# A loop over pairs of strips, written out strip by strip, in the sampling stage of a deformable convolution

## The reference

```
fine_cal  = conv1x1(gn(x) * (attn + 1), select_w)
align     = conv1x1(concat[fine_cal, 2 * coarse_up], offset_w)
om        = conv3x3(align, om_w, om_b)              # 216 channels: 8 groups x 9 taps x (dy, dx, mask)
val       = for each pixel, group and tap: bilinear sample of coarse_up at (y+ky+dy, x+kx+dx), times sigmoid(mask)
aligned   = einsum(val (9 taps x 256 channels), dcn_w) + dcn_b
out       = x + relu(aligned) + fine_cal
```

## Time and profile before

| | |
|---|---|
| median of 3 runs | 3370.52 us (3359.72 to 3374.48) |
| the profiled execution, its own time | 3370.08 us |
| its span in the trace | 3368.4 us |
| TensorE busy, weight loads busy | 3117.9 us (93%), 2697.5 us (80%) |
| VectorE, ScalarE, GpSimd busy | 2515.5 us (75%), 1517.4 us (45%), 335.5 us (10%) |
| mean granted TensorE clock | 0.967 |
| the sampling stage | from about 1205 us to the end |

### The profile page before, as it was taken

How to read it: one execution, slowest core, us unless ns; L and a number is a source line. 1 busy time by engine, 2 the same in 40 slices (tenths; PEclk the granted TensorE clock), 3 DMA queues, 4 the chain that set the end, 5 groups by cost and what they waited for, 6 DMA issues and landing times.

```text
span 3368.4 us, 91473 instructions
## 1 busy us (share of the span) xinstructions
PE 3117.9 (93%) x34242; PEld 2697.5 (80%) x34242; DVE 2515.5 (75%) x4215; ACT 1517.4 (45%) x2787; POOL 335.5 (10%) x445
## 2 busy tenths in 40 slices
PE   8969999999999938999998999998999998999999
PEld 7859999989999827878776777777777786877788
DVE  3427888888888859878776877887787786878782
ACT  0012222222222116656655565665666565656663
POOL 2000000000000001111111111111111111111111
PEclk9979999999999969999999999999999999999999
DMA  5322344333333232322223222223222233322222
GB/s 165 100 88 73 58 69 71 60 47 52 61 58 55 30 60 43 62 58 61 55 62 58 60 54 64 63 53 68 53 60 54 61 65 55 64 55 61 54 62 57
DMA packets 452882, 211.30 MB, mean 63 GB/s; under 512 B 230821, under 2 KB 447541, under 8 KB 452277
## 3 DMA queue, kind: packets, MB, share of 16 engines
q1 hardware_dynamic: 426112, 161.74, 26.6%
q10 hardware_dynamic: 21724, 26.37, 2.4%
q0 software_dynamic: 4608, 16.78, 1.3%
HBM read 104.86 MB, written 55.23 MB: 48 GB/s over the span
## 4 chain that ended last, share of the span: by engine, by line
PE 48%; ACT 7%; issue 6%; DVE 2%; ACTq 1%; SPq 1%; DMA 0%; POOL 0%; DVEq 0%; POOLq 0%
PE eb L1555 26%; PE tb L1113 14%; PE vb L1135 6%; ACT taps_all L1084 2%; ACT res L1142 1%; ACT wtT L1118 1%; ACT om L1040 1%; PE eb L1148 1%; PE tb L1035 1%; ACTq L1006 1%; DVE wt L1107 1%; ACT mask L1049 1%; ACT ot L1153 0%; SPq L1030 0%; ACTq L1435 0%
## 5 line engine op out<-in xcount | busy, mean ns | idle before, releaser
L1555 PE MATMUL eb<-val,wd 128*128 128x256 f32 (+1 forms) x4680 | 1225.7, 385 | 0.0
L1118 ACT COPY wtT<-tb 128x512 f32<-128x512 f32 x1152 | 662.7, 587 | 682.2 <-PE tb L1113 680.8
L1555 PEld LDWEIGHTS eb<-val,wd 128*128 128x128 f32 x4680 | 798.4, 191 | 120.8 <-issue 57.4
L1113 PE MATMUL tb<-ident,wt 128*128 128x128 f32 x4608 | 710.2, 278 | 85.7 <-issue 37.0
L1113 PEld LDWEIGHTS tb<-ident,wt 128*128 128x128 f32 x4608 | 564.7, 143 | 239.6 <-issue 77.1
L1107 DVE TENSOR_TENSOR wt<-taps_all 128x768 f32<-128x768 f32 x768 | 731.4, 994 | 10.4 <-PE tb L1113 2.1
L547 PE MATMUL conv<-fine,wf 128*108 128x256 f32 x4608 | 593.5, 290 | 13.1 <-DVE omT L878 13.1
L547 PEld LDWEIGHTS conv<-fine,wf 128*108 128x108 f32 x4608 | 572.8, 174 | 28.7 <-issue 28.7
L1488 DVE COPY val<-vb 128x432 f32<-128x432 f32 (+1 forms) x384 | 212.7, 554 | 240.4 <-PE vb L1135 240.1
L1135 PE MATMUL vb<-wtT,win 64*32 64x144 f32 x16384 | 323.3, 292 | 60.7 <-issue 56.4
L1135 PEld LDWEIGHTS vb<-wtT,win 64*32 64x32 f32 x16384 | 245.6, 108 | 108.5 <-issue 108.0
(11 more groups left out here) (142 smaller groups left out, 2499.8 us busy)
## 6 DMA issues: line engine op xcount, KB each, us to landing
val<-val SPq DMA_DIRECT2D x128, 396.0 KB, 3.8
win<-cpad SPq DMA_DIRECT2D x304, 64.0 KB
om_s<-om_d SPq DMA_DIRECT2D x1152, 12.0 KB
chunk<-in_x SPq DMA_DIRECT2D x32, 512.0 KB, 5.0
xchunk<-in_x SPq DMA_DIRECT2D x32, 512.0 KB, 4.1
r_d<-r POOLq DMA_DIRECT2D x32, 512.0 KB, 3.2
rt<-r_d SPq DMA_DIRECT2D x63, 256.0 KB, 4.9
out<-ot ACTq DMA_DIRECT2D x63, 256.0 KB, 2.9
```

The lines of the kernel that those rows point to most:

```text
L1113: last = nc.tensor.transpose(tb[b][:, 128 * j:128 * j + 128], wt[half][:, 4 * i + j, :], ident[:])
L1118: return nc.scalar.copy(dst, src) if e == "act" else nc.vector.tensor_copy(dst, src)
L1555: done = nc.tensor.matmul(eb[q][:, 256 * fo:256 * fo + rows], wd[:, half, k, 128 * fo:128 * fo + 128], val[:, half, k, at:at + rows // W, ...
```

## The change

The loop of `loop` goes: all 34 values of `it` are written out, for TensorE, VectorE and ScalarE. Each `strips(it)` issues the same work in the same order as before.

```
             def loop(e, strips):
 
-                strips(0)
-                strips(1)
-                with e.Fori(2, ST // 2 - 1) as it:
-                    strips(it)
-                for it in range(ST // 2 - 1, ST // 2 + 2):
+                for it in range(ST // 2 + 2):
                     strips(it)
```

## The result

The changed kernel takes 3281.79 us (median of 4 runs, 3280.20 to 3283.52) against 3369.99 us before (4 runs, 3359.72 to 3374.48): ratio 0.9743, 95% interval [0.9720, 0.9765], 88 us less. Forecast were 3277 us and a range of 3258 to 3305.

What follows compares the result with a forecast made beforehand. TensorE, busy 3117.9 of 3368.4 us, was taken to set the end. From 3370.1 us, 97.4 for jumps was subtracted and 4 for stops in written-out code added: 3276.7, so 3277 us, range 3258 to 3305.

Steps and rivals of the forecast that it cites:

- steps 1 and 3: TensorE's 28 loop jumps in the sampling stage: 136.4 us excess, of which 97.4 us goes, 3.48 us a jump.
- step 4: Bursts in written-out code on TensorE: 7 or 8 short stops of 0.57 us in 56 strips, adding about 4 us.
- step 2: First strips of images 1 to 3: TensorE's waits for window loads remain, so 39.0 us of the excess stays.
- pairs take over 61.5 us without an image's first strip: Sign in the sampling stage that the prediction is wrong; two strips were expected to take 60.8 us throughout.
- step 5: VectorE and ScalarE lose jumps and register instructions: nothing gained, since TensorE has the work; VectorE's smallest cover is 0.83 us.
- step 3: Sampling stage: 97.4 us goes, covering both gaps, the slow clock behind them and few jumps with another engine late.
- step 6: SyncE and GpSimd keep their loops at no cost: SyncE's wait falls to 11.7 us a strip, GpSimd has 5.1 spare.
- A: Rival, chance 0.07: written-out code stops more often; 3337 us with a stop in every slot, 3305 with one every strip.
- B: Rival, chance 0.04: another engine, such as VectorE, becomes the bound in the stage; 3366 us, or 3319 at half the slots.
- C: Rival, chance 0.01: TensorE's blocks come late in long code, at most 196 packets at 1.01 us, 198 us; 3471 us.
- D: Rival, chance 0.02: the gap at the turn of a pair is not the jump's; 3370 us, or 3367.
- E: Rival, chance 0.02: without gaps TensorE is throttled, half speed in a tenth of the stage losing some 100 us; 3377 us.

Runs made afterwards that it cites:

- the loops of one pass: Kernel before, with each pair of strips 4 to 61 written out in its own single-pass loop; 3281.84 us, ratio 0.9751.
- the kernel with the windows by half: Changed kernel, with each image's first-strip windows loaded in two parts, the left half's blocks earlier; 3241.59 us, ratio 0.9609 to the kernel before.

## Why the prediction was right

**The jumps (steps 1 and 3)** held. Predicted 97.4 us off the 56 strips before step 4, that is 93.4 after it; measured 91.3. The pair without a jump is 60.84 us over the stage instead of the 60.76 that I read from two strips, 28 x 0.08 = 2.2 us; this is about the whole miss within the stage. It is TensorE's jump, and by the packets its fetch, as the text said: 13 jumps cost 3.2 us each as 28 cost 3.15, and TensorE's alone give everything. Two of its arguments were weaker than they read. The exit of the earlier trace rows could not tell whose jump it was, since VectorE and ScalarE leave their loops there too; the runs with one side written out did. And the list of waits, "in keeping" with 97.4 us, holds 93.4 - 34.6 for the three long waits, or 59 us; of the rest a part was no wait at all but busy time, of which 28.3 us went.

**The stay of the three waits (step 2)** held: 42.28, 44.44 and 43.91 us for the two slots around them, 130.6 in all, against 130.1 before.

**The stops in written-out code (step 4)**: predicted 7 or 8 of 0.57 us, 4.3 us; measured 4 of 0.46 to 1.14 us, 3.3 us. Fewer but longer: that the sum came out close is luck; a rate from one event in 7.5 strips could not be better. The three pairs that hold the longer stops took 61.8 to 61.9 us, so by its letter the sign "pairs take over 61.5 us without an image's first strip" was met three times, by the stops of step 4 and by nothing else.

**VectorE and ScalarE (step 5)**: the price of zero was right and the reason given for it was the lesser half. I took their jumps to be like TensorE's and covered. The runs show no stop of theirs over two strips, and over four one that is covered. Likewise "the few jumps at which another engine was late", in step 3, did not exist: the kernel in which VectorE has no jumps shows more of such rows, not fewer.

**SyncE and GpSimd (step 6)** held: 11.7 us of waiting left per strip was computed, 11.8 measured, and writing them out changes nothing.

**The rest of the difference** lies outside the step that was forecast. The profiled execution after, 3283.52 us, is 6.8 us over the sum of 3276.7: 2.1 in the 56 strips, and 3.8 that the first of them begins later (1390.66 instead of 1386.86), 0.9 behind them. The last such matmuls ahead of the stage were already 2.9 us later (1206.93 against 1204.03), in code that was not touched. In the profiles of the nine experiments, which don't touch it either, the same matmul starts between 1201.86 and 1207.64 us, earliest with the loops of one pass: that is the spread of runs.

**The rivals.** A (many stops): 4 in 56 strips. B (another bound): 60.84 us a pair with VectorE waiting 0.79 us before its last copy of a slot. C (slower by late blocks) needed 0.50 us a packet; 3.3 us over 28 x 7 packets are 0.02. D (not the jump): the pairs of the loop over four that have no jump take 60.74 us, with all stores and copies at their turns. E (clock): 0.99 granted over the 56 strips, and 1.00 in the kernel with the windows by half, where the three waits are gone too.

## What to carry to other kernels

Compare a pass of a loop with the same work written out elsewhere in the same trace, and the two ends of the loop with each other: what a jump costs can be read before anything is changed. Here only the engine that sets the end paid, and its body was one that is fetched again in each pass; write out that one first (TensorE alone gave the whole 2.5%). Once the period is even, the few long waits left at the outer loop's turns stand out, and here loading the part that is free early was worth 40 us, issuing the same loads faster 8. A wait's label is a guess: ask whether the work it names was needed. And look at what a kernel made for an experiment really contains: the instruction count in its page showed that the loops of one pass had lost their arithmetic.

## What the runs showed of the hardware

- A jump back on TensorE, over a body of 1634 load and matmul records, cost 3.15 us in the mean of 28: a gap of some 2 us, mostly a second of about 1 us before the next burst, and at ten of the 28 jumps a stretch of 3.4 to 6.8 us at the lower clock.
- VectorE's and ScalarE's jump cost no stop and no fetch that shows, with 157 and 180 records in the body; with 312 and 358, and TensorE written out, VectorE stopped 13 times for 1.9 us in the mean (24.8 us), ScalarE was 2.2 us late at the jump looked at, and q14 moved 225 packets over the execution instead of 91. So what they keep is, as an estimate from these, more than 180 instructions and less than 312. The Trainium skill ("Runtime: NRT & Kernel Launch", section "Instruction fetch mechanics") speaks of blocks of 16 KiB, 256 instructions, and a window of two. TensorE's packets agree (5.67 MB in 346); those of the other queue are half as large (1.84 MB in 225). Two of these would hold 256 instructions, an estimate by the page's figure, and that lies between the two bodies.
- The label of a wait can be wrong by a whole mechanism: the same gap at TensorE's jump was put down to "issue" at most jumps, to VectorE at 3 and to ScalarE at 5 of 28 in the kernel before, and to VectorE at 12 once VectorE had no jump at all.
- Instruction blocks can come late in written-out code too, four times in 56 strips, by up to 1.14 us, each time at TensorE's fastest instructions or right behind them. What decides when was not tried.
